# A recurrent two-layer kernel on one core: gate on the attended values and low part of the query on VectorE, high part of the query on ScalarE, new instruction orders

## The reference, cut to what matters

```python
x = L0_attn_inputs
xn = _layernorm(x)
Q = K = V = xn @ Wq + bq                                  # per sequence
s = softmax(Q @ K.T / sqrt(128)) @ V                      # attended values
Y = einsum('tznp,npH->tzH', C, Y_tilde)                   # combine, C = softmax over experts
x = x + s * silu(Y)
...
# second layer: xn = layernorm(x); decay and input gates, scan over the sequence,
# rmsnorm, W_out, times silu(feed-forward), added to x
```

## Time and profile before

| | us |
|---|---|
| median of 3 runs | 1173.37 (1172.84 to 1174.8) |
| the profiled execution, its own time | 1174.86 |
| its span (first to last instruction) | 1172.8 |
| TensorE busy | 1146.9 (98%) |
| VectorE busy | 1024.4 (87%) |
| ScalarE busy | 1005.0 (86%) |
| GpSimd busy | 963.5 (82%) |

### The profile page before, as it was taken

The page is one execution under the profiler, slowest core; times in us unless marked ns, Lnnn a source line. Parts: engine busy times, 40 slices in busy tenths (PEclk is TensorE's granted clock), DMA queues, the critical chain, the costliest instruction groups (busy, mean ns, idle before and its releaser), DMA issues. The chain is left out here.

```text
span 1172.8 us, 17892 instructions
## 1 busy us (share of the span) xinstructions
PE 1146.9 (98%) x5165; PEld 796.6 (68%) x5165; DVE 1024.4 (87%) x1504; ACT 1005.0 (86%) x2349; POOL 963.5 (82%) x770
## 2 busy tenths in 40 slices
PE   7999999999999999999889999999999999999996
PEld 5666666666666666666367777777777777777773
DVE  7999999999999999999666877888887888888887
ACT  6989989877766666666568999999999999999998
POOL 3899999999999999999688877878777878777751
PEclk9999999999999999999999999999999999999999
DMA  4535435335333433343744444343444443444420
GB/s 133 178 145 194 163 129 198 149 125 185 140 143 122 162 139 142 124 162 139 246 160 154 131 145 144 123 141 126 133 144 144 134 137 126 127 144 144 140 77 19
DMA packets 125265, 167.39 MB, mean 143 GB/s; under 512 B 7536, under 2 KB 102000, under 8 KB 125040
## 3 DMA queue, kind: packets, MB, share of 16 engines
q1 hardware_dynamic: 123984, 165.71, 41.2%
q10 hardware_dynamic: 1184, 0.53, 0.2%
HBM read 90.71 MB, written 75.50 MB: 142 GB/s over the span
## 5 line engine op out<-in xcount | busy, mean ns | idle before, releaser
L146 POOL TENSOR_TENSOR exp_slots_loaded<-exp_slots_loaded,slot_max 128x1024 f32<-128x1024 f32 x128 | 330.6, 2600 | 9.1 <-DMA exp_slots_loaded<-exp_slots 7.3
L908 POOL TENSOR_TENSOR dd<-ed,rz 128x512 f32<-128x512 f32 x256 | 265.2, 1052 | 32.7 <-ACT rz L732 32.7
L579 PE MATMUL acc<-dd,xns 128*128 128x512 f32 x512 | 261.3, 592 | 0.7 <-POOL dd L908 0.7
L1967 DVE TENSOR_TENSOR clo<-ct,chi 128x512 fp32r<-128x512 f32 x256 | 170.3, 681 | 31.8 <-ACT chi L1635 30.7
L701 ACT ACTIVATE ed<-lg 128x512 f32<-128x512 f32 x256 | 140.9, 595 | 51.4 <-PE lg L556 50.4
L845 DVE TENSOR_REDUCE mr<-lg 128x16 fp32r<-128x512 f32 x256 | 169.3, 688 | 13.3 <-PE lg L520 9.1
L176 POOL TENSOR_TENSOR ch<-exp_slots_loaded 128x512 f32<-128x512 f32 x128 | 164.2, 1283 | 12.4 <-ACT exp_slots_loaded L710 12.4
L710 ACT ACTIVATE exp_slots_loaded<-lg 128x512 f32<-128x512 f32 x256 | 141.7, 593 | 29.1 <-PE lg L565 25.7
L861 DVE TENSOR_REDUCE zd<-ed 128x32 f32<-128x1024 f32 x128 | 155.3, 1213 | 1.3 <-ACT ed L701 1.3
L854 DVE TENSOR_REDUCE mr<-lg 128x32 fp32r<-128x1024 f32 x128 | 155.9, 1218 | 0.0
L1635 ACT ACTIVATE chi<-ct 128x512 fp32r<-128x512 f32 x256 | 147.5, 597 | 7.5 <-PE ct L1269 5.3
(11 more groups left out here) (328 smaller groups left out, 2507.4 us busy)
## 6 DMA issues: line engine op xcount, KB each, us to landing
exp_slots<-exp_slots_loaded SPq DMA_DIRECT2D x128, 512.0 KB, 2.9
exp_slots_loaded<-exp_slots SPq DMA_DIRECT2D x128, 512.0 KB, 3.5
xns<-xn_rows SPq DMA_DIRECT2D x128, 64.0 KB, 1.9
b_xraw<-in_xT SPq DMA_DIRECT2D x16, 256.0 KB, 3.6
out_t<-b_ti SPq DMA_DIRECT2D x15, 256.0 KB, 2.0
expert_w_late<-in_expert_w SPq DMA_DIRECT2D x5, 512.0 KB, 10.1
xn_rows<-slot_sum SPq DMA_DIRECT2D x8, 256.0 KB, 2.6
expert_w_early<-in_expert_w SPq DMA_DIRECT2D x3, 512.0 KB, 6.3
```

Source lines behind the costliest of these rows:

```text
L146: e.tensor_tensor(rows, rows, joined(SM, b)[:, h].unsqueeze(2).broadcast_to([P, TPB, GC * EPC, NP]), ALU.mult).then_inc(s_we)
L579: e.matmul(acc[k][:, :], xns[v % RX][:, :], dd[v % RX][:, bank(k)], start=tile == 0, stop=tile == NT - 1, skip_group_check=True).then_inc( ...
L908: e.tensor_tensor(dd[v % RX][:, bank(k)].rearrange("q (n p) -> q n p", p=NP), ed[v % RD][:, bank(k)].rearrange("q (n p) -> q n p", p=NP), ...
L1967: e.tensor_tensor(clo[g % RC][:, :], ct[c % 2][:, :], hi_f32(chi[g % RC][:, :]), ALU.subtract).then_inc(c_l)
```

## The change

It does the following, in phase 2 only.

1. `attended` (ScalarE, copy of `at[0]` to `st`) is gone, with its semaphore `o_c`. `gate_attended` moves from GpSimd to VectorE and reads `at[0]` itself. `project` of the next block, which writes `at[0]`, now waits for `gate_attended` (`us`) where it waited for `attended`.
2. `project_split` moves from VectorE to ScalarE and reads `at[0]` with the bias, ahead of `query`. `query_low` moves from GpSimd to VectorE and reads `at[0]` with the bias; it waits for `project_split` and `query`. `scores(0)`, which writes `at[0]`, waits for it too.
3. The orders of all five lists are new, in the loops and in the lists of the last block.

```diff
@@ sync2
                 for i in range(-2, NB + 3):
+                    exps(i + 1, 3)
                     load_x(i)
                     exps(i + 1, 2)
+                    exps(i + 1, 5)
                     exps(i + 1, 4)
-                    exps(i + 1, 3)
-                    exps(i + 1, 5)
                     exps(i + 1, 6)
@@ tensor2
-                            e.wait_ge(S["o_c"], i)
+                            e.wait_ge(S["us"], i)
                         three(at[0][:, :], W_Q, tiles_of(i, 0), tiles_of(i, 1)).then_inc(S["q_p"])
...
                         e.wait_ge(S["q_f"], i + 1)
+                        e.wait_ge(S["q_l"], i + 1)
@@ tensor2, loop
+                    exps_turned(i - 2, 13)
                     turn(i - 2, 1)
-                    exps_turned(i - 2, 13)
                     exps_turned(i - 2, 14)
+                    combine(i - 2, 12)
                     weigh(i - 2, 0)
-                    combine(i - 2, 12)
...
+                    ffn_k(i - 3)
                     input_gate(i - 3)
-                    exps_turned(i - 1, 2)
-                    exps_turned(i - 1, 3)
                     project(i - 1)
                     combine(i - 1, 0)
+                    exps_turned(i - 1, 2)
+                    input_product(i - 3)
                     combine(i - 1, 1)
-                    ffn_k(i - 3)
-                    input_product(i - 3)
+                    exps_turned(i - 1, 3)
                     values(i - 1)
                     exps_turned(i - 1, 4)
                     scores(i - 1, 0)
@@ scalar2
+                def project_split(i):
+                    if within(i):
+                        e.wait_ge(S["q_p"], i + 1)
+                        if i:
+                            e.wait_ge(A["s"], i * TPB)
+                        e.activation(R["qh"][:, :], at[0][:, :], ACT.Identity, bias=one(VEC, V_BQ)).then_inc(S["q_h"])
...
-                def attended(i):
-                    if within(i):
-                        e.wait_ge(A["w"], (i + 1) * TPB)
-                        if i:
-                            e.wait_ge(S["us"], i)
-                        e.activation(B["st"][:, :], at[0][:, :], ACT.Copy).then_inc(S["o_c"])
@@ scalar2, loop
                     chunk_high(i - 1, 8)
                     log_table(i - 1)
+                    chunk_high(i - 1, 9)
                     state_log(i - 3)
-                    scaled(i - 1, 2)
-                    state_inverse(i - 3)
-                    chunk_high(i - 1, 9)
...
                     decay_tanh(i - 2)
+                    turn_high(i - 1, 3)
                     decay(i - 2)
-                    decay_squares(i - 2)
-                    turn_high(i - 1, 3)
                     chunk_high(i, 1)
                     y_tanh(i - 1)
+                    decay_squares(i - 2)
                     log_table(i - 1)
-                    attended(i - 1)
                     input_log(i - 2)
                     tanh_table(i - 1)
+                    project_split(i)
                     query(i)
                     chunk_high(i, 2)
+                    input_tanh(i - 2)
                     chunk_high(i, 3)
-                    input_tanh(i - 2)
+                    value_high(i)
                     ffn_k_relu(i - 2)
-                    value_high(i)
@@ vector2
+                def gate_attended(i):
+                    if within(i) and i < LAST:
+                        e.wait_ge(S["u_y"], i + 1)
+                        e.wait_ge(A["w"], (i + 1) * TPB)
+                        e.tensor_tensor(B["ty"][:, :], B["ty"][:, :], at[0][:, :], ALU.mult).then_inc(S["us"])
+
+                def query_low(i):
+                    if within(i):
+                        e.wait_ge(S["q_f"], i + 1)
+                        e.wait_ge(S["q_h"], i + 1)
+                        e.scalar_tensor_tensor(R["ql"][:, :], at[0][:, :], one(VEC, V_BQ), hi_f32(R["qh"][:, :]), ALU.add,
+                                               ALU.subtract).then_inc(S["q_l"])
@@ vector2, loop
                     chunk_low(i - 1, 12)
+                    gate_second(i - 3)
                     output(i - 3)
                     normalise(i - 2)
                     turn_low(i - 1, 1)
...
                     chunk_low(i - 1, 14)
-                    mix_k(i - 2)
                     turn_low(i - 1, 2)
                     chunk_low(i - 1, 15)
                     chunk_low(i, 0)
                     mix_r(i - 2)
+                    next_max(i + 1)
+                    mix_k(i - 2)
                     turn_low(i - 1, 3)
                     chunk_low(i, 1)
-                    next_max(i + 1)
+                    silu_y(i - 1)
                     one_minus(i - 2)
-                    silu_y(i - 1)
+                    gate_attended(i - 1)
                     residual(i - 1)
-                    project_split(i)
+                    query_low(i)
                     chunk_low(i, 2)
+                    gated(i - 2)
                     chunk_low(i, 3)
-                    gated(i - 2)
                     value_low(i)
                     row_max(i, 0)
@@ gpsimd2, loop
-                    gate_attended(i)
-                    query_low(i + 1)
                     exps_weighed(i + 1, 3)
                     next_sums(i + 2)
                     exps_weighed(i + 1, 4)
                     exps_weighed(i + 1, 5)
+                    exps_weighed(i + 1, 6)
                     next_weights(i + 2)
-                    exps_weighed(i + 1, 6)
```

More of the change, by code:

```diff
@@ L1523, in tensor2 @@
                     exps_turned(i - 1, 10)
+                    combine(i - 1, 8)
                     mean(i - 2)
-                    combine(i - 1, 8)
+                    state_out(i - 3)
                     combine(i - 1, 9)
@@ L1533, in tensor2 @@
                 combine(LAST, 10)
-                combine(LAST, 11)
                 exps_turned(LAST, 13)
                 turn(LAST, 1)
+                combine(LAST, 11)
+                weigh(LAST, 0)
                 exps_turned(LAST, 14)
-                weigh(LAST, 0)
+                turn(LAST, 2)
                 combine(LAST, 12)
-                turn(LAST, 2)
-                weigh(LAST, 1)
                 combine(LAST, 13)
                 exps_turned(LAST, 15)
+                turn(LAST, 3)
                 decay_gate(LAST - 1)
-                turn(LAST, 3)
+                weigh(LAST, 1)
                 combine(LAST, 14)
```

127 lines of the change are left out of this document (56 added, 71 removed).

## The result

The changed kernel takes 1182.45 us (median, 1181.31 to 1186.84) against 1174.42 us for the kernel before on the same chip: a ratio of 1.0083, 95% interval 1.007 to 1.0096. It is slower, by 8.0 us where 2.8 were forecast, and outside the range.

A forecast was written before the change was run, and what follows sets the result against it. The prediction took TensorE as the bound, waiting about 0.3 us of a 35.05 us body. Its terms, 4.9 - 2.1 + 0 = +2.8 us, on the median of 1173.37 gave 1176.2 us, range 1170.0 to 1180.0.

The forecast's parts named there:

- What bounds the kernel: TensorE, judged by distances between starts: it waits about 0.3 us in a body of 35.05 us.
- `exps_turned` 4: Transposes on TensorE wait for `chunk_low` 2 behind ScalarE's later `query`: +0.35 us in 14 bodies, +4.9 us.
- Rival (a): The wait at `exps_turned` 4 does not form, leaving block 0's gain: 1171.3 us; chance 0.25.
- Rival (c): VectorE's `value_low` is too late for `scores` 1, 0.35 us more in each block: 1181.1 us; chance 0.12.
- Block 0: Start of phase 2: `exps_turned` 4 starts 1.4 us earlier, chunk 9's copy 0.7 earlier; together -2.1 us.
- Chunk 9's copy: In block 0, a copy TensorE waits for loses one activation ahead of it: -0.7 us (0 to -0.8).
- Rival (d): Block 0's gain is absent or taken back, with the wait at `exps_turned` 4 in place: 1178.3 us; chance 0.11.
- The last block: Same operations in another order, ScalarE loses nothing: 0 us, with 1 us either way.
- `project`: TensorE's `project` waits 0 to 0.2 us for VectorE's `gate_attended`, a wait that does not add.
- the old wait at `turn` 2: TensorE's existing wait of 0.3 us a body, behind `normalise` and a table load, stays.
- The step that failed: GpSimd loses two operations of about 1.30 us a block, worth nothing mid-phase 2; later load 2 also taken as nought.
- a GpSimd weighing or a load among TensorE's waits: Sign in the profile after that would make the prediction wrong in its ground.

The follow-up runs named there:

- e11: The changed kernel with the fourth weighing behind the scan, `decay` and `decay_squares` earlier on ScalarE, `exps_turned` 4 behind `scores` 0 on TensorE: 1175.35 us, ratio 1.0007.

## Why the prediction was wrong

*What bounds the kernel.* Right, and it stayed so: TensorE by its distances, and every us lost was lost where TensorE waits.

*`exps_turned` 4.* Right in mechanism, place and size. Forecast: `query` 5.05 us behind `y_tanh`, transposes 0.15 us behind the end of `chunk_low` 2, +0.35 us in each of 14 bodies. Measured: 687.18 to 692.23 is 5.05; the transposes start at 694.44, 0.15 us after 693.61 + 0.68; bodies +0.39. The run with `decay_squares` ahead of `y_tanh` showed the chain named in the forecast to be the cause, for about half of the amount, and the run with the query ahead of the table load showed the rest to sit in the same chain, since there the transposes wait no longer. Rival (a) is refuted. Rival (c) was named as the next in line, and that is what it was: as soon as `exps_turned` 4 was out of the way, `scores` 1 waited for `value_low`.

*Block 0.* The start was right: -1.36 for -1.4, and the kernel with only TensorE's new order shows it alone. Chunk 9's copy came 0.8 us earlier behind `values` 0 (10.79 instead of 11.59), 0.7 forecast, yet bodies 0 and 1 together became only 0.38 shorter; that term was too large, as half of it is lost again before body 1 ends. Rival (d) is refuted.

*The last block.* Forecast 0. In the kernel without long scans it is 0.46 us longer, about what the one wait at `exps_turned` 4 in it makes. Right. The further 1.25 us of the changed kernel are its long scan.

*`project` and the old wait at `turn` 2.* No wait of `project` in the full bodies, and none that adds; `turn` 2 still starts 0.34 us behind the product ahead of it. Right.

With these terms at their measured sizes the sum is 14 x 0.39 - 1.36 - 0.38 + 0.1 = +3.8 us, the 0.1 being what the last block has beyond its 0.39; the kernel with the weighing behind the scan is 3.5 us above before. That would have been within the range.

*The step that failed* is the one on GpSimd, "No weighing of exponentials ends a TensorE wait in the middle of phase 2, so this is worth nothing there", together with what I did with the new SyncE order: I asked only whether a later load makes a weighing late for TensorE, and took nought. In the loop the weighings were never late. They acted through VectorE, whose durations I had taken as fixed: a weighing that starts at the same time as an operation of VectorE with two operands in SBUF makes that operation wait until it has ended. I had named "a GpSimd weighing or a load among TensorE's waits" as what would break the forecast, and even that was looked for in the wrong place: the table of waits shows VectorE's `clo`, one step removed.

The trace of the kernel before did show the effect. Its scan, DVE in a full body, in the last block, and in the body after it where GpSimd does no weighing:

```profile
876.76 1.47 DVE L2070 TENSOR_TENSOR_SCAN b_hh<-b_aa,vectors,b_ti 128x512 f32<-128x512 f32 x1
...
1122.01 2.18 DVE L2070 TENSOR_TENSOR_SCAN b_hh<-b_aa,vectors,b_ti 128x512 f32<-128x512 f32 x1
...
1156.19 1.28 DVE L2070 TENSOR_TENSOR_SCAN b_hh<-b_aa,vectors,b_ti 128x512 f32<-128x512 f32 x1
```
```profile
876.69 0.46 POOL L130 TENSOR_TENSOR slot_joined<-slot_sum 128x128 f32<-128x128 f32 x1
877.11 3.31 POOL L146 TENSOR_TENSOR exp_slots_loaded<-exp_slots_loaded,slot_max 128x1024 f32<-128x1024 f32 x1
...
1120.72 5.65 POOL L146 TENSOR_TENSOR exp_slots_loaded<-exp_slots_loaded,slot_max 128x1024 f32<-128x1024 f32 x2 [0.63 <-DVE b_ti L2062]
```

The scan has three durations in one kernel, 1.28 alone, 1.47 behind a small operation of GpSimd that began 0.07 us before it, 2.18 behind a weighing that began 1.28 us before it; and the weighing at 877.11, which began 0.35 us behind the scan, takes 3.31 where the others take 2.38. A group of one line whose mean hides such a spread is a warning. From there the right question was: what decides the order of scan and fourth weighing? Before, the weighing follows the joined sums on GpSimd and comes 0.35 us behind the scan, in every full body. After, it follows whichever comes last, the joined sums or the landing of load 4, and starts between 0.09 us ahead and 2.2 us behind. Half of the price could have been worked out too. In the first of these rows the scan ends 1.08 us behind the end of the GpSimd operation that was first (877.15 to 878.23), so by estimate a weighing of 2.38 us that starts with it makes it end 2.2 us later. That TensorE feels 1.5 of this, no row of the kernel before shows.

The Trainium skill ("SBUF — State Buffer", section "🔬 SBUF: two separate sides") states it as a rule: VectorE and GpSimd share a pair of ports to SBUF as an exclusive lock that an instruction holds to its end, also when the VectorE operation has two inputs in SBUF and the GpSimd one reads it, and the one that starts first keeps the other out. The runs agree, in both directions: 3.40 to 3.47 us for 1.27 when GpSimd is first, up to 3.44 for 2.38 when VectorE is.

What stays open: why load 4 lands up to 2.2 us apart from body to body, and where the last 0.24 us of the query's chain would go if it were freed on both sides of the table load. Neither was tried. That GpSimd's operation is what the scan waits for is shown; that the ports are the means is the Trainium skill's account, which the runs agree with and don't test.

## What to carry to other kernels

Before you move work or loads between queues, list every VectorE operation with two SBUF operands and look which GpSimd operation starts within its length of time; the order of the two starts is a hidden dependency, and an edit on a third queue (here SyncE's loads) can turn it over. Where the VectorE operation is on the bound's path, let the GpSimd one wait for it: here that wait cost nothing and gave 4 us back. And look for what stands ahead of a moved operation in the queue that it leaves or joins: the two kernels with the gate behind a weighing behind a late load were 25.5 and 49 us slower than before (the second with its long scans), though the gate lasts 1.3 us.

## What the runs showed of the hardware

- The scan (128 x 512, float32, two operands in SBUF) lasts 1.27 us alone and 3.37 to 3.47 us if a GpSimd operation of 2.38 us begins between 0.09 us ahead and 0.01 us behind it. Begun 0.37 us ahead, it makes the scan 3.09 us, begun 1.28 ahead, 2.18. At 0.03 us behind, the scan lasts 1.27 and the GpSimd operation 3.44. I had not expected that 0.02 us would decide 2.2.
- The edge is sharp, and lies a little behind a tie. In the kernels with TensorE's new start and with the moves alone, a GpSimd operation of 0.46 us (L130) begins 0.02 or 0.03 us behind the scan. In 15 bodies, at 17 to 25 ns, the scan lasts 1.55 to 1.56 us and it 0.46. In 11, at 25 to 32 ns, the scan lasts 1.27 and it 1.49 to 1.51. DVE and POOL of one of the 11, from the moves alone:

```profile
774.44 1.27 DVE L2077 TENSOR_TENSOR_SCAN b_hh<-b_aa,vectors,b_ti 128x512 f32<-128x512 f32 x1
```
```profile
774.46 1.50 POOL L130 TENSOR_TENSOR slot_joined<-slot_sum 128x128 f32<-128x128 f32 x1
```

- The one that waits ends behind the end of the one that was first by its own length less about 0.2 us: the scan 1.08 us behind in every such row (1.27 alone), the weighing 2.19 (2.38 alone), `residual` 0.54 (0.69 alone).
- The length of the waiting operation follows the other's remainder more than its own size: a maximum of 128 columns took 2.50 us instead of 0.28, and `residual` 2.92 instead of 0.69.

The last one, DVE and POOL of the run with `exps_turned` 4 and `decay_squares` both moved (e11). `query_low` stands behind it and starts at 729.75, when its own input has just come (729.72), so that TensorE loses nothing:

```profile
726.78 2.92 DVE L2016 SCALAR_TENSOR_TENSOR b_x<-b_ty,b_xraw 128x512 f32<-128x512 f32 x1
```
```profile
726.75 2.41 POOL L146 TENSOR_TENSOR exp_slots_loaded<-exp_slots_loaded,slot_max 128x1024 f32<-128x1024 f32 x1 [4.62 <-DMA exp_slots_loaded<-exp_slots]
```

- Operations of VectorE that read one operand from a bank kept their length beside the same weighings: `clo` lasts 0.66 to 0.69 us in all of its 256 rows of the changed kernel, with a weighing beside it or without.
